# A fourth group of attention weights split into fp16 pairs, with reordered rows, positions and ScalarE work, in a graph attention and mixture-of-experts kernel

## The reference

```python
x = x + gnn(layernorm(x))            # 4096 x 256
#   Wh = x @ W ; e = leaky_relu(e_src[:, None] + e_dst[None, :], 0.2)
#   e = where(adj > 0 | eye, e, -9e15) ; P = softmax(e, axis=1) ; h = P @ Wh
x = x + ffn(layernorm(x))
#   logits = x @ Wr + br ; the two largest of 8 experts, gates renormalised
#   y_e = gelu((LN(x) * g_e + b_e) @ W1_e + b1_e) @ W2_e + b2_e   (256 -> 1024 -> 256)
```

## Time and profile before

| what | value |
|---|---|
| median of 3 runs | 990.39 us (988.03 to 991.64) |
| the profiled execution, its own time | 994.33 us |
| its span, first to last instruction | 992.4 us |
| TensorE busy | 950.7 us (96%) |
| VectorE busy | 788.8 us (79%) |
| ScalarE busy | 615.4 us (62%) |
| GpSimd busy | 622.0 us (63%) |

### The profile page before, as it was taken

One profiled execution on the slowest core, in us unless ns is written; L12 is line 12 of the kernel. 1 busy time (PEld: TensorE's weight loads), 2 busy tenths in 40 slices (PEclk: granted clock), 3 DMA queues, 4 the chain that ended last, 5 costly groups with the idle time before them and its releaser, 6 DMA issues. The chain is left out here.

```text
span 992.4 us, 22974 instructions
## 1 busy us (share of the span) xinstructions
PE 950.7 (96%) x7562; PEld 799.7 (81%) x7563; DVE 788.8 (79%) x1199; ACT 615.4 (62%) x905; POOL 622.0 (63%) x630
## 2 busy tenths in 40 slices
PE   6999999999999999999999999999999999999994
PEld 5788999989988889888888977777777777777762
DVE  6789989999999999999999446787666666577653
ACT  4889898788888887878786554433333433333441
POOL 5221251486674964847629458888888888888652
PEclk9999999999999999999999999999999999999998
DMA  8658878688787787886877986443332332232321
GB/s 265 134 159 254 269 237 272 205 256 242 223 260 271 221 258 244 236 270 181 264 240 202 352 336 212 94 110 62 61 55 44 48 58 43 43 52 46 44 35 22
DMA packets 92636, 170.71 MB, mean 172 GB/s; under 512 B 20480, under 2 KB 69888, under 8 KB 84224
## 3 DMA queue, kind: packets, MB, share of 16 engines
q1 hardware_dynamic: 57984, 133.54, 40.3%
q0 software_dynamic: 24048, 26.23, 17.0%
q10 hardware_dynamic: 10512, 9.72, 3.4%
HBM read 136.65 MB, written 41.19 MB: 179 GB/s over the span
## 5 line engine op out<-in xcount | busy, mean ns | idle before, releaser
L1162 ACT ACTIVATE hf<-tp,b_cols 128x256 f32<-128x256 f32 (+1 forms) x312 | 116.4, 460 | 176.1 <-PE tp L903 173.7
L795 PE MATMUL acc<-wh,pt_hi 128*128 128x256 f16 x768 | 209.3, 273 | 0.0
L796 PE MATMUL acc<-wh,pt_hi 128*128 128x256 f16 x768 | 209.3, 273 | 0.0
L797 PE MATMUL acc<-wh,pt_lo 128*128 128x256 f16 x768 | 209.3, 273 | 0.0
L559 POOL TENSOR_TENSOR x_late<-x_late,wsp 128x1024 f32<-128x1024 f32 x32 | 78.9, 2464 | 178.2 <-DMA x_late<-in_L_ffn_W 173.0
L919 PE MATMUL acc<-w_sb,h_hi 128*128 x568 | 170.9, 379 | 5.1 <-issue 3.8
L1294 DVE SCALAR_TENSOR_TENSOR sc<-t_row,s_col 128x2048 f32<-128x2048 f32 x64 | 166.4, 2599 | 9.1 <-PE tp L776 6.9
L901 PE MATMUL tp<-x_hi,w_sb 128*128 128x256 f16 (+1 forms) x624 | 161.2, 264 | 1.9 <-ACT hf L1162 1.8
L665 POOL DMA_INDIRECT out<-y_sb,yidx x71 | 120.9, 1703 | 65.2 <-DVE y_sb L1617 38.1
L903 PE MATMUL tp<-x_down,w_sb 128*128 128x256 f16 (+1 forms) x624 | 161.2, 264 | 0.0
L902 PE MATMUL tp<-x_lo,w_sb 128*128 128x256 f16 (+1 forms) x624 | 160.8, 263 | 0.0
(11 more groups left out here) (238 smaller groups left out, 1779.4 us busy)
## 6 DMA issues: line engine op xcount, KB each, us to landing
adj_sb<-in_adj SPq DMA_DIRECT2D x64, 1024.0 KB, 7.5
x_late<-in_L_ffn_W SPq DMA_DIRECT2D x32, 512.0 KB, 9.8
wsplit_dram<-wsp SPq DMA_DIRECT2D x32, 512.0 KB, 7.3
w_sb<-wsplit_dram SPq DMA_DIRECT2D x32, 512.0 KB, 8.7
xs<-rows_dram ACTq DMA_DIRECT2D x32, 260.0 KB, 3.4
wsp<-in_L_ffn_W POOLq DMA_DIRECT2D x32, 256.0 KB, 4.9
x<-in_x SPq DMA_DIRECT2D x32, 128.0 KB, 10.5
out<-x SPq DMA_DIRECT2D x32, 128.0 KB
```

Of the source, the lines that this page charges most:

```text
L795: pe.matmul(o, pt_hi[g][:, cols], wh[:, j, 0, :], start=(j == 0), stop=False)
L796: pe.matmul(o, pt_hi[g][:, cols], wh[:, j, 1, :], start=False, stop=False)
L797: m = pe.matmul(o, pt_lo[g][:, cols], wh[:, j, 0, :], start=False, stop=False)
```

## The change

Group 3 of P is now split into two fp16 parts as the others are. The high part is `p_hi` again. For the low part TensorE multiplies the high part by a matrix `minus` (-1/1024 on its diagonal, made by GpSimd at the start) and adds it onto the transposed values that still lie in `tp1` (`subtract_high`), and ScalarE copies the remainder out (`p_rest`). `Wh` has two fp16 parts for all columns, so VectorE has a `wh_lo` for four more pairs. In the FFN tail (one-half tiles) successive tiles use the two `acc` banks in turn (`bank_of`), and `down` waits for the y before last; in the written-out tiles `down` uses the register that `up` has loaded. On ScalarE, `p_rest(i - 1)` comes first, `mask` moves ahead of `p_hi(i, 1)`, and `w_scaled` and `normalise` move behind `p_hi(i, 3)`. On TensorE, `av(i - 1, 2)` moves ahead of the transposes of group 1, and `router_pos` behind the subtraction. On VectorE the first two rows are normalised before the statistics of rows 4 to 7. SyncE's program is as it was.

```diff
@@ -518,6 +521,8 @@
                       allow_small_or_imprecise_dtypes=True).then_inc(s_pc, 1)
             pool.iota(dest[:, :], [[P, T]], base=0, channel_multiplier=1,
                       allow_small_or_imprecise_dtypes=True).then_inc(s_pc, 1)
+            pool.wait_ge(s_pc, 1)
+            pool.tensor_scalar(minus[:, :], ident[:, :], -1.0 / PSCALE, 0.0, ALU.mult, ALU.add).then_inc(s_pc, 1)
 
             def scales(m):
                 cols = slice(batches[m][0], batches[m][0] + batches[m][1])
...
@@ -741,7 +746,7 @@
                     pe.wait_ge(s_tr, 2 * NP)
                 if j > 2:
                     pe.wait_ge(s_whh, max(2, 2 * (j - 3)))
-                    pe.wait_ge(s_whl, max(2, 2 * sum(lows[:j - 3])))
+                    pe.wait_ge(s_whl, max(2, 2 * (j - 3)))
                 for h in range(2):
                     o = banks(j)[0][h]
                     for k in range(KD):
...
@@ -766,14 +771,15 @@
                 if g == 0 and i > 0:
                     pe.wait_ge(s_lo, GS * i)
                 if g == 1 and i > 0:
-                    pe.wait_ge(s_hi, G * i)
+                    pe.wait_ge(s_lq, i)
                 if g == 1 and i == 0:
-                    pe.wait_ge(s_whl, 2 * sum(lows[:NP - 1]))
+                    pe.wait_ge(s_whl, T - 2)
                     pe.wait_ge(s_whh, T - 2)
                 if g > 1:
                     pe.wait_ge(s_lo, GS * i + g - 1)
                 for c in range(GJ):
-                    m = pe.transpose(tp[g % 2][:, c * P:(c + 1) * P], sc[u][:, (GJ * g + c) * P:(GJ * g + c + 1) * P], ident[:, :])
+                    m = pe.matmul(tp[g % 2][:, c * P:(c + 1) * P], sc[u][:, (GJ * g + c) * P:(GJ * g + c + 1) * P], ident[:, :],
+                                  is_transpose=True, start=(g < GS or c % (GJ // 2) == 0), stop=True, skip_group_check=True)
                 m.then_inc(s_t, 1)
 
             def av(i, u, g):
...
@@ -782,22 +788,27 @@
                 if g < GS:
                     pe.wait_ge(s_lo, GS * i + g + 1)
                 else:
-                    pe.wait_ge(s_hi, G * i + G)
+                    pe.wait_ge(s_lq, i + 1)
                 if g == 0 and within(i, 2, T):
                     pe.wait_ge(s_x1, X1 * (i - 2) + 3)
                 if g == 1 and i == 0:
-                    pe.wait_ge(s_whl, TS)
+                    pe.wait_ge(s_whl, T)
                     pe.wait_ge(s_whh, T)
                 for c in range(GJ):
                     j = GJ * g + c
                     cols = slice(c * P, (c + 1) * P)
-                    if g < GS:
-                        pe.matmul(o, pt_hi[g][:, cols], wh[:, j, 0, :], start=(j == 0), stop=False)
-                        pe.matmul(o, pt_hi[g][:, cols], wh[:, j, 1, :], start=False, stop=False)
-                        m = pe.matmul(o, pt_lo[g][:, cols], wh[:, j, 0, :], start=False, stop=False)
-                    else:
-                        m = pe.matmul(o, pt32[:, cols], wh32[:, c, :], start=False, stop=(c == GJ - 1))
+                    pe.matmul(o, pt_hi[g][:, cols], wh[:, j, 0, :], start=(j == 0), stop=False)
+                    pe.matmul(o, pt_hi[g][:, cols], wh[:, j, 1, :], start=False, stop=False)
+                    m = pe.matmul(o, pt_lo[g][:, cols], wh[:, j, 0, :], start=False, stop=(j == T - 1))
                 m.then_inc(s_av, 1)
+
+            def subtract_high(i):
+
+                pe.wait_ge(s_hi, G * i + G)
+                for h in range(2):
+                    cols = slice(h * GW // 2, (h + 1) * GW // 2)
+                    m = pe.matmul(tp[1][:, cols], minus[:, :], pt_hi[GS][:, cols], start=False, stop=True, skip_group_check=True)
+                m.then_inc(s_sub, 1)
 
             def router_t(b, h):
                 pe.wait_ge(s_row, RB * b + 2 * h + 2)
...
@@ -839,9 +850,11 @@
                     p_transpose(i, u, 0)
                     if i == 0:
                         project(NP - 1)
+                if i > 0:
+                    av(i - 1, 1 - u, 2)
+                if now:
                     p_transpose(i, u, 1)
                 if i > 0:
-                    av(i - 1, 1 - u, 2)
                     av(i - 1, 1 - u, 3)
                 if in_batch(b) and q == 2:
                     router_t(b, 0)
...
@@ -851,15 +864,16 @@
                 if in_batch(b) and q == 2:
                     router_mm(b, 0)
                     router_t(b, 1)
-                if in_batch(b) and q == 3:
-                    router_pos(b)
                 if now:
                     p_transpose(i, u, 3)
                     av(i, u, 1)
+                    subtract_high(i)
+                if in_batch(b) and q == 3:
+                    router_pos(b)
                 if in_batch(b) and q == 2:
                     router_mm(b, 1)
 
-            pe.wait_ge(s_whl, 2 * sum(lows[:NP - 2]))
+            pe.wait_ge(s_whl, T - 4)
             pe.wait_ge(s_whh, T - 4)
             for i in range(T):
                 attend(i)
...
@@ -905,9 +923,12 @@
                         m.then_inc(s_g1, 1)
 
             def down(t, u):
-                e = expert_of(t)
+                e = experts.pop(t) if isinstance(t, int) and t in experts else expert_of(t)
+                a = bank_of(t)
                 pe.wait_ge(s_hh, t + 1)
-                if within(t, 1, FT):
+                if within(t, NB + 1, FT) and isinstance(t, int):
+                    pe.wait_ge(s_yc, total(t - 1, 2))
+                elif within(t, 1, FT):
                     pe.wait_ge(s_yc, total(t, 2))
                 else:
                     pe.wait_ge(s_x1, X1 * (T - 1) + 3)
...
@@ -916,10 +937,10 @@
                     w_both = w_blocks[:, bass.ds(e * CHUNKS + 2 + c // 4, 1), :, (c % 4) * D:(c % 4 + 1) * D].rearrange("p a z n -> p (a z) n")
                     w_hi = w_both[:, 0, :]
                     for s in range(ns):
-                        pe.matmul(acc[s][:, :], h_hi[u][:, (c * ns + s) * P:(c * ns + s + 1) * P], w_both,
+                        pe.matmul(acc[s + a][:, :], h_hi[u][:, (c * ns + s) * P:(c * ns + s + 1) * P], w_both,
                                   start=(c == 0), stop=False, skip_group_check=True)
                     for s in range(ns):
-                        m = pe.matmul(acc[s][:, 0:D], h_lo[u][:, (c * ns + s) * P:(c * ns + s + 1) * P], w_hi,
+                        m = pe.matmul(acc[s + a][:, 0:D], h_lo[u][:, (c * ns + s) * P:(c * ns + s + 1) * P], w_hi,
                                       start=False, stop=(c == HC - 1), skip_group_check=True)
                 m.then_inc(s_down, 1)
 
...
@@ -1025,8 +1046,13 @@
                 act.wait_ge(s_t, G * i + g + 1)
                 if within(i, 1, T):
                     act.wait_ge(s_av, G * i + g - 3)
-                dst = pt_hi[g] if g < GS else pt32
-                act.activation(dst[:, :], tp[g % 2][:, :], ACT.Copy, scale=PSCALE).then_inc(s_hi, 1)
+                act.activation(pt_hi[g][:, :], tp[g % 2][:, :], ACT.Copy, scale=PSCALE).then_inc(s_hi, 1)
+
+            def p_rest(i):
+                act.wait_ge(s_sub, i + 1)
+                if within(i, 1, T):
+                    act.wait_ge(s_av, G * i)
+                act.activation(pt_lo[GS][:, :], tp[1][:, :], ACT.Copy, scale=PSCALE).then_inc(s_lq, 1)
 
             def normalise(b, k):
 
...
@@ -1090,33 +1116,36 @@
                 u, b, q = i % 2, i // RB - 1, i % RB
                 now = i < T
                 ahead = i + 2 < T
+                if i > 0:
+                    p_rest(i - 1)
                 if now:
                     p_hi(i, 0)
-                    if i == 0:
-                        wh_hi(NP - 1)
+                if i == 0:
+                    wh_hi(NP - 1)
                     p_hi(i, 1)
-                if i == 0:
                     first_step()
                     return
                 if ahead:
                     mask(i + 2, u, 0)
+                if now:
+                    p_hi(i, 1)
                 if i < T - 1:
                     exps(i + 1, 1 - u, 0)
                     exps(i + 1, 1 - u, 1)
-                if in_batch(b) and q == 1:
-                    for k in range(RB):
-                        normalise(b, k)
                 if in_batch(b) and q == 2:
                     router(b, 0)
                 if now:
                     p_hi(i, 2)
-                    w_scaled(i)
                 if ahead:
                     mask(i + 2, u, 1)
                 if in_batch(b) and q == 2:
                     router(b, 1)
                 if now:
                     p_hi(i, 3)
+                    w_scaled(i)
+                if in_batch(b) and q == 1:
+                    for k in range(RB):
+                        normalise(b, k)
                 if i == T - 2:
                     load_first()
                 if in_batch(b) and q == 3:
...
@@ -1239,11 +1269,13 @@
 
             next_stats(0, 4)
             moments(0)
+            scaled_by(0)
+            normalise(0)
+            normalise(1)
             next_stats(4, 8)
```

(33 more changed lines are left out.)

9 lines of the change are left out of this document (4 added, 5 removed).

## The result

| | before | after |
|---|---|---|
| median, beside each other | 991.01 us (988.03 to 994.30, 4 runs) | 1007.96 us (1005.44 to 1008.93, 4 runs) |
| the profiled execution, its span | 994.33, 992.4 us | 1008.93, 1007.1 us |

The ratio is 1.0161, with a 95% interval of 1.0144 to 1.0179: slower by 16 us (the two medians lie 17 apart). The forecast was 998, with a range up to 1007. The direction was right, and so was the mechanism that it put first, the late load; the size was not.

What follows compares the result with a forecast made beforehand. TensorE was taken to bound attention, VectorE close behind. From the profiled 994.3 us: -13.1 - 14.2 + 7.7 + 27 + 3.7 - 3.3 = 1002.1, then 998 because the runs' median lies 3.9 us below that execution; range 980 to 1007.

Steps and rivals of the forecast that it cites:

- the late load: Late normalise delays SyncE's x1 load and the adjacency load behind it; masks, then TensorE, wait in six batches: +27 us.
- Old waits and group 3: Attention on TensorE: fp16 group 3 -13.1 us, old waits gone -14.2, new lateness of VectorE +7.7.
- The tile of 14.4 us: TensorE's time for a plain attention tile with group 3 in fp16, 0.41 us less than before.
- Rival 2: VectorE bounds attention, so TensorE's saving in 24 router-batch tiles may come to nothing: +10 us, 1008; chance 0.11.
- Front: Before and in the first attention tiles: later first transposes +1.6 us, waits in tiles 0 and 1 +2.1, together +3.7.
- Tail: Last tiles: the kept register saves seven reads of the expert on TensorE, -3.3 us; the two banks nothing.
- rival 3: ScalarE bounds every attention tile, losing say 0.5 us a tile: +16 us, 1014; chance 0.07.
- the slack of 0.8 us: Plain tile: ScalarE's copies and mask end 0.8 us before TensorE reaches the subtraction, so TensorE does not wait.

Runs made afterwards that it cites:

- E5: Kernel before, GpSimd's subtraction for the expert weights cut to one column, leaving out nearly all their low parts: 977.32 us, ratio 0.9841.
- E6: Kernel before, group 3 of P multiplied with half of the columns of Wh, so TensorE has less work: 989.95 us, ratio 0.9963.
- F2: Kernel before with F1's edit of GpSimd's program alone: 978.36 us, ratio 0.9864.
- E2: Changed kernel, normalise still late, SyncE issues the x1 load one step later, behind both adjacency halves: 986.42 us, ratio 0.9944.
- F1: E2 with GpSimd's w_rest held for the mask sum of the next tile but one, row_scales and cast_w ahead of it: 965.34 us, ratio 0.9734.
- F3: E2 with E5's one-column subtraction on GpSimd: 965.06 us, ratio 0.9730.
- E4: Kernel before with one edit, normalise moved behind p_hi(i, 3) on ScalarE: 1003.08 us, ratio 1.0116.
- E1: Changed kernel with normalise back in its earlier place behind the exponentials on ScalarE: 993.27 us, ratio 1.0016.
- F4: Changed kernel with E5's one-column subtraction on GpSimd: 1004.73 us, ratio 1.0135.
- G1: F4 with 28 fp16 matmuls, results unread, added ahead of router_mm in each router tile: 990.62 us, ratio 0.9988.
- E8: Kernel before with the tail's edits of the change alone (banks in turn, kept register, later wait of down): 990.17 us, ratio 0.9974.

## Why the prediction missed

**What bounds the kernel: the step that failed.** "So TensorE bounds attention with VectorE close behind" was read from 62.77 and 61.77 us of 64.68. E5 and E6 turn it round, and F2 confirms it with nothing left out: TensorE's work is 62.2 us a batch, and it was VectorE that made the batch 64.7. Its busy time alone doesn't say so. The cause lay in GpSimd, and I looked only at each engine's own work: ten of the scores in the trace before take 3.0 to 4.5 us instead of 2.34. I had seen the mean and not the two forms in it. All scores take 166.4 us before and 150.1 in E5, and four short operations of the expert choice 13.0 us less between them: VectorE's busy time held some 29 us in which GpSimd blocked it. E5 was 16.0 us faster.

The Trainium skill ("SBUF — State Buffer", Who interferes with whom) states the rule that would have told it: a VectorE instruction with two inputs in SBUF and a GpSimd instruction that reads SBUF contend for a shared port, an exclusive lock, while one with at most one SBUF input, outside VectorE's two-port modes, does not contend. The rows agree. Scores and mask sum read two SBUF tensors and are stretched; `p_lo` reads PSUM and one SBUF tensor and keeps its 1.20 us with a `w_rest` on top.

**Old waits and group 3: -13.1 - 14.2 + 7.7 = -19.6 forecast, -9.7 measured** (attention in E2, 441.7 against 451.4 us). The tile of 14.4 us was right, and F1 and F3 reach 60.65 us a batch with it. In the real kernel it met VectorE, whose mask sums became 12.8 us longer. That is a second effect of the late rows, and the prediction had no term for it: mask sums are stretched where the rows stand late, with TensorE's old order too (E4), and not where they stand early (E1). The rows at tile 9 show how: GpSimd's scatter comes to lie under the scores, ends 1.6 us later than it would alone, and `w_rest` behind it meets the mask sum. Why the late rows shift the scores against the scatter wasn't tried. Rival 2 named the bound and priced it at +10 us, 1008; price and total came out, its cause (VectorE's work alone) was only part of it. I gave it 0.11.

**The late load: +27 forecast, +21.5 measured** (E2). Right in place, in number and in chain. The masks waited 3.6 us on average where 4.6 were laid out, because the loads landed at the short end. That the size is close is partly luck: uncovered, the same late load costs 39.7 us (F4), of which 17 are a clock that I left out (G1), and VectorE's lateness hid nearly half.

**Front: +3.7 forecast, +3.0 measured** (mask sum of tile 3 at 93.70 instead of 90.68). The first transposes start at 63.93, where I had 64.6; TensorE waits 1.59 us for `p_rest(0)`, where I had 1.7. **Tail: -3.3 forecast, -3.2 measured** (E8, interval 0.9 to 4.4); in the two profiles the stretch from the experts' third tile on is 2.3 us shorter with the change. **ScalarE** (rival 3): TensorE waits for `pt_hi` at the subtraction once, 0.70 us; the slack of 0.8 us was real, and E1 shows it used up.

**The sum again**, all terms from the profiles: +21.4 for the late load (attention 463.1 against 441.7 in E2), -9.7, +3.0 in the front, -2.3 in the tail, and +2.3 between the last mask sum and the experts' third tile (51.9 us instead of 49.6), where the last mask sum is stretched by 2.6 us. That is the 14.7 between the two spans. The range ended at 1007 because rival 2 was kept out of it when two chances in ten had to be left.

## What to carry to other kernels

Two engines within 2% of each other in busy time aren't ranked by it: relieve each by itself and see which one moves the end, and look for two durations of one instruction before trusting its mean. A wait hidden in a queue is priced by who is late at that moment, so one stall had prices from 12 to 40 us here; the change lost until the blocked load stood behind the adjacency loads in SyncE's queue, and was worth 13 us (F1 against F2) once GpSimd's work lay under VectorE's PSUM reads. Both were smaller edits than the change.
